# Moving set-up work of a linear attention into the loop before it, and reordering the opening of two joined attentions

## The chip, the cores and the metric

One Trainium2 chip, one core. The metric is the device time of one execution in microseconds; the median over the runs is compared. A core has five engines with their own instruction queues: TensorE (PE in the profile, its weight loads PEld), VectorE (DVE), ScalarE (ACT), GpSimd (POOL) and SyncE (SP). They meet only at semaphores: an instruction waits until a counter has reached a value that another engine's instructions raise.

## The reference

The input x has 32 sequences of 64 tokens with 128 channels, 2048 rows of 128 in all, which the kernel keeps in SBUF as 16 tiles of 128 rows. Six layers follow, each a sum of x and something of its layer norm (`_ln` here): a cross attention with 16 wide heads, a linear attention with an MLP, a mixture of four small self attentions in which each token takes part in two, a cross attention with 16 heads of 8 channels, an attention with relative positions, and a causal attention with a mixture of MLPs.

```python
x = x + cross_wide(_ln(x), ctx)                  # stage_cross_wide
x = x + linear_and_mlp(_ln(x))                   # stage_linear, stage_mlp
x = x + experts_attention(_ln(x))                # stage_two_attentions, first half
x = x + cross_narrow(_ln(x), ctx, mask)          # stage_two_attentions, second half
x = x + relative_attention(_ln(x))
x = x + causal_attention_and_moe(_ln(x))

# linear_and_mlp(x), x already normalised; rms(x, s) = x * s * (sqrt(128) + 1e-6) / |x|
q, k, v = split(rms(x, scale1) @ qkv_w.T);  q, k = exp(-q*q/2), exp(-k*k/2)
out = q @ (k.T @ v) / (q @ k.sum + 1e-6)         # per head
x = x + gamma * (out @ proj_w.T + proj_b)
return x + gamma * (gelu(rms(x, scale2) @ conv1_w.T + conv1_b) @ conv2_w.T + conv2_b)

# experts_attention(x): logits = x @ router_w + router_b; probs = softmax(logits)
# top2 experts of each token; for each expert, attention among its tokens; summed with weight probs
```

## The kernel before

The stages run one after another (`stages` in `build`). Each stage is an `nc.Block` with one instruction stream per engine, written out by hand; between two blocks all engines meet. No planner orders the work: an engine does its stream in the order of the calls, and a call such as `phi(a)` starts with the waits that it needs. `run_units` (line 97) calls `step(a)` for each unit; inside it `a.plus(1)` or `a.plus(-2)` names the unit that a call works on, so that several units are in flight. Calls outside the range of units do nothing.

**`stage_cross_wide`** (line 482) works on units of 64 query rows, two to a tile, 32 in all. Per unit TensorE makes scores in PSUM, VectorE takes maxima, subtracts them and later sums (`at.shift`, lines 353 and 358, `sums`, line 702), ScalarE does the exponential (line 364), GpSimd multiplies with the reciprocal (`scale`, line 549), TensorE transposes (line 376), ScalarE copies (line 386), TensorE multiplies with the context and, for every second unit, with the output weights (line 636); `finish` (line 712) adds the result to X. VectorE and GpSimd have idle time in each unit. At the end the last tiles run without new units beside them.

**`stage_linear`** (line 736) works on 8 groups of two tiles. VectorE first makes weights scaled by gamma and scale1 (line 770, `scaled_weights`), `stats` of the first groups (lines 788 and 794), GpSimd `scales` (lines 877 to 881), VectorE `xnorm` (lines 805 and 807: the normalised rows Xmid and the doubly normalised rows xn), and only then TensorE's `turn` (line 977) can begin. In the loop a step is: `qkv` (lines 1006 and 1008), ScalarE's `phi` (lines 946 to 958), `sums` (line 988), VectorE's `mask` (line 818), `numer` (line 1020), `divide` (lines 831 to 837), `oturn`, `proj`, `mid`. GpSimd adds `biases` (line 890) and, in steps 2 to 6, makes `constants` that the joined attentions need later, among them the memset of Vbd (line 900) and the casts of `place` (line 910).

**`stage_mlp`** (line 1049) has 8 groups of two tiles as well. Beside them it makes the statistics of the next layer norm and in steps 4 and 6 the normalised rows of the first eight tiles (`next_rows`, line 1109). After it the semaphores are cleared.

**`stage_two_attentions`** (line 1300) begins with statistics and rows of the last tiles (`rows_ready`, line 1955), transposes of all rows in four groups of four tiles (`turn_rows`, line 1471, copied to XnT by ScalarE, line 1797), the router's products with N = 4 (`route`, line 1477), `keys(0)` (lines 1521 and 1768) and `queries(0)` (lines 1512 and 1842). VectorE ranks the logits (lines 1971 to 1982, `rank_columns`), TensorE turns the one-hot rows (`turn_hot`, line 1485), ScalarE copies them; `selections` (lines 1501 and 1793) spreads them, GpSimd multiplies queries (`select`, line 1361) and keys (`keys`, line 1370) with them, `values` (lines 1533 and 1777) follow, and the first `score` (lines 1549 and 1556) and `shift` (lines 1853 and 1856). Then comes a loop of 32 units, whose `normalise` takes a reciprocal (line 1940), makes a factor from it (line 1942) and multiplies the mixed values with it (line 1946).

## Time and profile before

| | us |
|---|---|
| median of 3 runs | 1072.82 (1067.55 to 1075.33) |
| the profiled execution: its time | 1074.42 |
| the profiled execution: its span | 1072.3 |

```profile
span 1072.3 us, 26858 instructions
PE 960.8 (90%) x10835; PEld 730.2 (68%) x10835; DVE 658.4 (61%) x1312; ACT 519.3 (48%) x1071; POOL 462.0 (43%) x517
PE   4899999999867787999999999997999788699994
PEclk9999999999978887999999999998999889699997
```

The span reaches from the first to the last instruction; the time has some microseconds around it. The second line gives each engine's busy time, its share of the span and its instructions. The last two cut the span into 40 slices of 26.8 us: a digit is the busy share of TensorE in tenths, and the TensorE clock that was granted, in tenths of 2.4 GHz. The cross attention lies in slices 2 to 12, the linear attention and the MLP in 12 to 15, the joined attentions from 15 on.

### The profile page before, as it was taken

To read this page: it belongs to the slowest core of one execution; us is meant where nothing else is said; L and a number is where in the kernel's file an instruction comes from. 1 tells how busy PE (TensorE), PEld (TensorE's weight loads), DVE (VectorE), ACT (ScalarE), POOL (GpSimd) and SP (SyncE) were. 2 spreads that over 40 slices of the span, in tenths; PEclk is the share of its full clock that TensorE was granted. 3 is DMA by queue.
4 is the path that set the end of the run, shared out by engine and by line. 5 is a ranking of instruction groups with operands and counts; after the bars stand their busy time and mean duration, and the time that the engine had idled before them with its cause. 6 is when DMAs were issued, how large, how long until landed. Compare 5 with 4: busy or idle time off the path is not lost. (4 is left out here: it accounts for less than half of the span.)

```text
span 1072.3 us, 26858 instructions
## 1 busy us (share of the span) xinstructions
PE 960.8 (90%) x10835; PEld 730.2 (68%) x10835; DVE 658.4 (61%) x1312; ACT 519.3 (48%) x1071; POOL 462.0 (43%) x517
## 2 busy tenths in 40 slices
PE   4899999999867787999999999997999788699994
PEld 4788888888645576888888666664356545567773
DVE  3355555555526673877889788874589757722324
ACT  2464555555414433666666566663455438242231
POOL 1123233332215453766767534423145266356243
PEclk9999999999978887999999999998999889699997
DMA  9300034000000000000000000003963010012336
GB/s 276 143 2 1 1 90 111 1 1 1 1 1 1 1 25 17 2 3 2 3 2 2 2 2 2 2 2 115 380 192 103 2 42 4 27 49 64 90 108 181
DMA packets 43369, 55.04 MB, mean 51 GB/s; under 512 B 4368, under 2 KB 34704, under 8 KB 42864
## 3 DMA queue, kind: packets, MB, share of 16 engines
q1 hardware_dynamic: 41264, 49.07, 14.5%
q0 software_dynamic: 1984, 4.26, 1.2%
q8 instruction: 87, 1.43, 0.5%
q14 instruction: 34, 0.28, 0.1%
HBM read 30.13 MB, written 23.19 MB: 50 GB/s over the span
## 5 line engine op out<-in xcount | busy, mean ns | idle before, releaser
L549 POOL TENSOR_TENSOR c_P<-c_P,c_rl 128x1024 f32<-128x1024 f32 x32 | 60.7, 1896 | 127.5 <-DVE c_rl L705 127.5
L1741 ACT COPY e_PT<-probsT 128x512 f32<-128x512 f32 x128 | 68.8, 591 | 81.2 <-PE probsT L1570 81.2
L602 PEld LDWEIGHTS mixed<-c_xs,c_AQ 128*128 128x128 f32 x512 | 66.1, 197 | 35.1 <-issue 33.4
L702 DVE TENSOR_REDUCE c_rl<-c_P 128x8 f32<-128x1024 f32 x32 | 39.0, 1220 | 81.9 <-ACT c_P L364 81.9
L1750 ACT ACTIVATE e_P<-e_P 128x512 f32<-128x512 f32 x128 | 74.6, 641 | 0.7 <-DVE e_P L1856 0.3
L602 PE MATMUL mixed<-c_xs,c_AQ 128*128 128x128 f32 x512 | 71.3, 286 | 2.9 <-ACT c_GT L667 1.6
L626 PE MATMUL mixed<-c_PT,c_cs 128*128 128x512 f32 x128 | 68.9, 620 | 4.5 <-ACT c_RT L676 3.1
L676 ACT COPY c_RT<-mixed 128x512 f32<-128x512 f32 x64 | 37.5, 586 | 63.1 <-PE mixed L626 63.1
L1570 PE MATMUL probsT<-W,e_P 128*128 128x128 f32 x512 | 67.5, 275 | 0.0
L636 PEld LDWEIGHTS mixed<-c_VO,c_RT 128*128 128x128 f32 x512 | 60.5, 198 | 5.3 <-ACT c_RT L676 5.3
L636 PE MATMUL mixed<-c_VO,c_RT 128*128 128x128 f32 x512 | 62.1, 282 | 2.0 <-ACT c_RT L676 2.0
L612 PE MATMUL scores<-ctxT,c_GT 128*128 128x128 f32 x512 | 63.3, 277 | 0.0
L353 DVE TENSOR_REDUCE c_mx<-scores 128x8 f32<-128x1024 f32 x32 | 38.5, 1204 | 38.7 <-PE scores L612 38.7
L612 PEld LDWEIGHTS scores<-ctxT,c_GT 128*128 128x128 f32 x512 | 59.6, 192 | 2.3 <-issue 2.3
L1570 PEld LDWEIGHTS probsT<-W,e_P 128*128 128x128 f32 x512 | 57.0, 141 | 0.6
L1853 DVE TENSOR_REDUCE e_mx<-scores 128x16 f32<-128x1024 f32 x32 | 39.2, 1224 | 25.4 <-PE scores L1556 25.4
L386 ACT COPY c_PT<-probsT 128x512 f32<-128x512 f32 x64 | 34.3, 593 | 41.1 <-PE probsT L376 41.1
L667 ACT COPY c_GT<-mixed 128x256 f32<-128x256 f32 x128 | 41.4, 375 | 26.4 <-PE mixed L602 26.4
L1661 PEld LDWEIGHTS mixed<-e_V,e_PT 128*64 128x64 f32 x1024 | 32.5, 138 | 26.4 <-ACT e_PT L1741 25.6
L1895 DVE TENSOR_REDUCE e_mx<-scores 128x8 f32<-128x1024 f32 x32 | 39.0, 1219 | 15.3 <-PE scores L1641 14.9
L2935 POOL DMA_INDIRECT hbm_results<-e_yo,e_ids x30 | 28.8, 959 | 44.1 <-DVE e_yo L2910 38.6
L2093 POOL TENSOR_TENSOR u_RK<-u_KT,W 128x1024 f32<-128x1024 f32 x16 | 30.4, 1902 | 39.3 <-PE scores L2170 36.5
(391 smaller groups left out, 2377.3 us busy)
## 6 DMA issues: line engine op xcount, KB each, us to landing
hbm_dist<-u_Z SPq DMA_DIRECT2D x16, 768.0 KB, 7.5
u_S<-hbm_dist SPq DMA_DIRECT2D x64, 128.0 KB, 2.9
hbm_results<-c_blank SPq DMA_DIRECT2D x1, 3072.0 KB, 14.4
e_w<-in_w SPq DMA_DIRECT2D x12, 256.0 KB, 2.7
e_dT<-hbm_results SPq DMA_DIRECT2D x12, 256.0 KB, 4.5
W<-in_wpack SPq DMA_DIRECT2D x1, 2489.0 KB, 12.8
hbm_slots<-c_blank SPq DMA_DIRECT2D x6, 350.0 KB, 5.9
e_xin<-hbm_slots SPq DMA_DIRECT2D x6, 350.0 KB, 3.6
```

The source lines that it names most:

```text
L549: pool.tensor_tensor(pr, pr, bc(rl[:, a.up, :].unsqueeze(2), [P, PAIRS, KEYS]), ALU.mult).then_inc(s["scaled"], 1)
L602: last = pe.matmul(bank[:, (h % 4) * P:(h % 4 + 1) * P], AQ[:, h, :], xs[:, a.par, :], start=True, stop=True)
L612: last = pe.matmul(K.psS[a.up][:, c * KEYS:(c + 1) * KEYS], GT[:, a.par, a.u, 2 * c:2 * c + 2, :].rearrange("p h q -> p (h q)"), K.ctxT[:, ...
L626: pe.matmul(K.psO[:, :], cs[:, a.up, :], at.PT[:, a.up, r * 512:(r + 1) * 512], start=True, stop=True).then_inc(s["read"], 1)
L636: last = pe.matmul(K.psO[:, 0:D], RT[:, a.par, h, :], VO[:, h, :], start=(h == 0), stop=(h == HEADS - 1))
L667: last = act.copy(GT[:, a.par, b, 4 * r:4 * r + 4, :], bank[:, :].rearrange("p (h b q) -> p h b q", h=4, b=TB)[:, :, b, :])
L702: dve.tensor_reduce(rl[:, a.up, :], at.P[:, a.up, :].rearrange("p (g k) -> p g k", g=PAIRS), AX.X, ALU.add).then_inc(s["chain"], 1)
L1570: last = pe.transpose(K.psT[:, i * P:(i + 1) * P], Pr[:, n % 2, i * P:(i + 1) * P], K.ident)
L1741: act.copy(PT[:, n % 2, half * 512:(half + 1) * 512], K.psT[:, half * 512:(half + 1) * 512]).then_inc(s["tcopied"], 1)
L1750: act.activation(Pr[:, n % 2, cols], Pr[:, n % 2, cols], ACT.Exp, scale=0.5 if n < TOTAL else CSCALE).then_inc(s["exped"], 1)
L1853: dve.tensor_reduce(top, sc, AX.X, ALU.max).then_inc(s["maxed"], 1)
L1895: dve.tensor_reduce(top, sc, AX.X, ALU.max).then_inc(s["maxed"], 1)
```

## The change

Three stages are touched.

1. Linear attention. The scaled weights, the ones and zeroes of vb, and for tiles 0 to 11 the statistics and scales are made in the loop of the cross attention (`linear_weights`, `group_stats`, `linear_scale`), in named steps, four tiles at a time; also the normalised rows of tiles 0 to 3 (`linear_rows`, steps 28 and 29). The last four tiles' statistics follow in step 0 of the linear attention, their scales in its step 1. `constants` moves from GpSimd's steps 2 to 6 of the linear attention to its steps 22 to 26 of the cross attention, unchanged but for the step numbers; onehot and identb move to VectorE's steps 5 and 7 there. TensorE's first two turns wait for nothing. The buffers concerned are reserved earlier.
2. MLP. TensorE transposes the first eight tiles' rows for the joined attentions (`next_turn`, steps 5 and 7), ScalarE copies them to XnT (`next_copy`), TensorE makes their router products (`next_route`, steps 6 and 8).
3. Joined attentions. The opening is reordered as the diff shows: keys first, only the last eight tiles turned and routed there, the hot rows ahead of the first queries' bias, the exponential of the logits behind the first values, the first score ahead of the second selection, the token weights behind the first shift. In `normalise` the reciprocal is written to a free column in PSUM instead of to the SBUF tile rl, which is gone.

```diff
+def linear_scale(pool, K, s, g, count):
+    L, tiles = K.L, slice(4 * g, 4 * g + 4)
+    var = L.mv[:, tiles, 1]
+    pool.wait_ge(s["var"], count)
+    pool.tensor_scalar(L.rs[:, 0, tiles], var, LN_EPS, None, ALU.add)
+    pool.tensor_scalar(L.rs[:, 1, tiles], var, D / RMS_NUM ** 2, None, ALU.mult).then_inc(s["vareps"], 1)
+    pool.wait_ge(s["vareps"], count)
+    pool.tensor_tensor(L.rs[:, :, tiles], L.rs[:, :, tiles], K.nhalf[:, 0:8].rearrange("p (a b) -> p a b", a=2),
+                       ALU.pow).then_inc(s["rs"], 1)
+def linear_rows(dve, K, n):
+    L = K.L
+    for i in range(2):
+        t = 2 * n + i
+        mean, row_in = L.mv[:, t, 0:1], K.X[:, t, :]
+        dve.tensor_scalar(K.Xmid[:, t, :], row_in, mean, L.rs[:, 0, t:t + 1], ALU.subtract, ALU.mult)
+        last = dve.tensor_scalar(L.xn[:, n % 2, i, :], row_in, mean, L.rs[:, 1, t:t + 1], ALU.subtract, ALU.mult)
+    return last
...
                     pool.tensor_copy(w(name), byhead[:, :, :, :, :].rearrange("p g j e d -> p (g j e d)")).then_inc(s["heads"], 1)
+                def constants(n):
...
                 def step(a):
                     if a.u == 0:
                         tile_in(a.plus(2 * U))
                     context(a.plus(1))
                     scale(a.plus(1))
+                    constants(a.n)
+                    if a.n in (11, 19, 27):
+                        linear_scale(pool, K, ln, (a.n - 11) // 8, (a.n - 11) // 8 + 1)
...
+                def linear_weights(n):
+                    gamma = K.row("gamma")
+                    if n == 9:
+                        dve.wait_ge(K.load["rest"], 16)
+                        dve.tensor_scalar(L.Wqkv[:, :], w("qkvT"), w("scale1"), None, ALU.mult)
+                        dve.memset(L.vb[:, :, :, :], 0.0).then_inc(ln["zeroed"], 1)
+                    if n == 11:
...
+                        dve.tensor_tensor(L.projG[:, :], w("projT"), gamma, ALU.mult)
+                        dve.tensor_tensor(L.projB[:, :], K.row("proj_b"), gamma, ALU.mult)
...
                 def step(a):
                     at.shift(dve, a.plus(1))
...
                     if a.u == 1:
                         finish(a.plus(-2))
+                    if a.n == 5:
+                        dve.tensor_reduce(K.onehot[:, :], K.ident.rearrange("p (r i) -> p i r", r=4), AX.X, ALU.add).then_inc(
+                            s["onehot"], 1)
+                    if a.n == 7:
+                        dve.tensor_copy(K.identb[:, :], K.ident)
+                    linear_weights(a.n)
+                    if a.n in (10, 18, 26):
+                        g = (a.n - 10) // 8
+                        dve.wait_ge(ln["xout"], 4 * (g + 1))
+                        group_stats(dve, ln, L.st6, L.mv, K.X, g)
+                    if a.n in (28, 29):
+                        dve.wait_ge(ln["rs"], 1)
+                        linear_rows(dve, K, a.n - 28)
...
+                    if a.n == GROUPS - 2:
+                        dve.wait_ge(s["rs"], 1)
+                    wait(dve, s["turned"], a.n - 1)
+                    linear_rows(dve, K, a.n).then_inc(s["xn"], 1)
+                def last_stats():
+                    for t in range(TILES - 4, TILES):
+                        last = dve.bn_stats(L.st6[:, t, :], K.X[:, t, :])
+                    last.then_inc(s["stats"], 1)
+                    dve.wait_ge(s["stats"], 1)
+                    for t in range(TILES - 4, TILES):
+                        last = dve.bn_aggr(L.mv[:, t, :], L.st6[:, t, :])
                     last.then_inc(s["var"], 1)
-                def xnorm(a):
...
-                    dve.wait_ge(s["rs"], a.n + 1)
...
                 def biases(a):
                     if not inside(a):
                         return
-                    pool.wait_ge(s["xn"], a.n + 1)
+                    wait(pool, s["xn"], a.n - 1)
...
                 def step(a):
-                    scales(a.plus(2))
                     biases(a)
...
-                pool.wait_ge(s["weights"], 6)
+                    if a.n == 1:
+                        linear_scale(pool, K, s, 3, 1)
...
                         return
-                    pe.wait_ge(s["xn"], a.n + 1)
+                    wait(pe, s["xn"], a.n - 1)
                     wait(pe, s["xnT"], a.n)
...
+                def next_copy(g):
+                    act.wait_ge(v["turned"], g + 1)
+                    act.copy(K.XnT[:, 512 * g:512 * g + 512], K.psM[:, :]).then_inc(v["copied"], 1)
...
                 def step(a):
                     gelu(a)
                     xT(a.plus(1))
+                    if a.n in (5, 7):
+                        next_copy((a.n - 5) // 2)
...
+                def next_turn(g):
+                    pe.wait_ge(v["normed"], g + 1)
+                    pe.wait_ge(v["boe"], 1)
+                    wait(pe, v["copied"], g)
+                    for i in range(4):
+                        last = pe.transpose(K.psM[:, i * P:(i + 1) * P], K.Xmid[:, 4 * g + i, :], K.ident)
+                    last.then_inc(v["turned"], 1)
+                def next_route(g):
+                    pe.wait_ge(v["copied"], g + 1)
+                    for t in range(4 * g, 4 * g + 4):
+                        pe.matmul(K.psO[:, t * E0:(t + 1) * E0], K.XnT[:, t * P:(t + 1) * P], w("rw"), start=True, stop=True)
...
                     if a.n == 1:
                         bias_products()
+                    if a.n in (5, 7):
+                        next_turn((a.n - 5) // 2)
+                    if a.n in (6, 8):
+                        next_route((a.n - 6) // 2)
...
-            keyed = lambda t: M if t else K.psO
+            keyed = lambda t: M if t else K.psS[0][:, 0:512]
+            turned_rows = lambda g: K.psS[1][:, 512 * (g - DONE):512 * (g - DONE) + 512]
...
-                    turn_rows(0)
-                    turn_rows(1)
-                    route(0)
                     keys(0)
+                    for g in range(DONE, groups):
+                        turn_rows(g)
+                    for g in range(DONE, groups):
+                        route(g)
                     queries(0)
-                    route(1)
-                    for g in range(2, groups):
-                        turn_rows(g)
-                    for g in range(2, groups):
-                        route(g)
                     turn_hot()
                     selections(0)
                     values(0)
+                    score(0)
                     selections(1)
                     queries(1)
-                    score(0)
                     keys(1)
                     for n in range(TOTAL):
...
-                    for g in range(groups):
-                        act.wait_ge(q["turned"], g + 1)
-                        act.copy(K.XnT[:, g * G * P:(g + 1) * G * P], K.psS[g % 2][:, 0:G * P]).then_inc(q["copied"], 1)
-                        if g == 1:
-                            keys(0)
-                    act.wait_ge(q["shifted"], 1)
-                    act.activation(ex[:, :, :], ex[:, :, :], ACT.Exp).then_inc(q["exped"], 1)
+                    keys(0)
+                    for g in range(DONE, groups):
+                        act.wait_ge(q["turned"], g + 1 - DONE)
+                        act.copy(K.XnT[:, g * G * P:(g + 1) * G * P], turned_rows(g)).then_inc(q["copied"], 1)
                     act.wait_ge(q["hotT"], 1)
                     act.copy(hotT[:, :, :], K.psT[:, 512:512 + 2 * P].rearrange("p (i q) -> p i q", i=2)).then_inc(q["hotTout"], 1)
                     selections(0)
                     values(0)
+                    act.wait_ge(q["shifted"], 1)
+                    act.activation(ex[:, :, :], ex[:, :, :], ACT.Exp).then_inc(q["exped"], 1)
                     selections(1)
                     keys(1)
                     for n in range(TOTAL):
...
                         wait(dve, s["normed"], n - 1)
                         ps = mixed(n)
-                        dve.reciprocal(rl[:, n % 2, :], ps[:, :, E0 * HD]).then_inc(s["recip"], 1)
+                        dve.reciprocal(ps[:, :, E0 * HD + 1], ps[:, :, E0 * HD]).then_inc(s["recip"], 1)
                         dve.wait_ge(s["recip"], n + 1)
-                        dve.tensor_tensor(fac[:, n % 2, :, :], bc(rl[:, n % 2, :].unsqueeze(2), [P, HEADS, E0]),
+                        dve.tensor_tensor(fac[:, n % 2, :, :], bc(ps[:, :, E0 * HD + 1:E0 * HD + 2], [P, HEADS, E0]),
                                           bc(wsel[:, t, k, :].unsqueeze(1), [P, HEADS, E0]), ALU.mult).then_inc(s["factor"], 1)
...
+                    def token_weights():
+                        dve.wait_ge(q["exped"], 1)
+                        ch.link(dve, dve.tensor_reduce(rx[:, :], ex[:, :, :], AX.X, ALU.add))
+                        ch.link(dve, dve.reciprocal(rx[:, :], rx[:, :]))
+                        ch.link(dve, dve.tensor_tensor(ex[:, :, :], ex[:, :, :], bc(rx[:, :].unsqueeze(2), [P, TILES, E0]), ALU.mult))
+                        for k in range(TOPK):
+                            last = dve.tensor_tensor(wsel[:, :, k, :], hot[:, :, k, :], ex[:, :, :], ALU.mult)
+                        ch.link(dve, last)
+                        dve.tensor_tensor(wtok[:, :, :], wsel[:, :, 0, :], wsel[:, :, 1, :], ALU.add).then_inc(q["weights"], 1)
...
-                    queries(0)
                     ch = Chain(q["chain"])
+                    dve.memset(less[:, :, :, :], 0.0)
                     dve.wait_ge(q["logits"], 1)
-                    ch.link(dve, dve.tensor_tensor(logits[:, :, :], K.psT[:, 512:512 + TILES * E0].rearrange("p (t e) -> p t e", t=TILES),
+                    ch.link(dve, dve.tensor_tensor(logits[:, :, :], K.psO[:, 0:TILES * E0].rearrange("p (t e) -> p t e", t=TILES),
...
-                    ch.link(dve, dve.tensor_reduce(rx[:, :], logits[:, :, :], AX.X, ALU.max))
-                    dve.tensor_tensor(ex[:, :, :], logits[:, :, :], bc(rx[:, :].unsqueeze(2), [P, TILES, E0]),
-                                      ALU.subtract).then_inc(q["shifted"], 1)
-                    rank_columns(dve, ch, rank[:, :, :], less, logits, E0)
+                    rank_columns(dve, ch, rank[:, :, :], less, logits, E0, False)
...
-                    dve.wait_ge(q["exped"], 1)
-                    ch.link(dve, dve.tensor_reduce(rx[:, :], ex[:, :, :], AX.X, ALU.add))
...
-                    ch.link(dve, last)
-                    dve.tensor_tensor(wtok[:, :, :], wsel[:, :, 0, :], wsel[:, :, 1, :], ALU.add).then_inc(q["weights"], 1)
+                    queries(0)
+                    ch.link(dve, dve.tensor_reduce(rx[:, :], logits[:, :, :], AX.X, ALU.max))
+                    dve.tensor_tensor(ex[:, :, :], logits[:, :, :], bc(rx[:, :].unsqueeze(2), [P, TILES, E0]),
+                                      ALU.subtract).then_inc(q["shifted"], 1)
...
                         shift(n)
+                        if n == 0:
+                            token_weights()
```

## Rows read from the trace of the kernel before

**Rows 1.** Windows: stretch, length, busy us of each engine (instructions), TensorE clock, DMA share, GB/s

```profile
240.00:260.00 20.00, 20.00 (x145) 16.65 (x143) 10.71 (x12) 11.34 (x25) 4.97 (x6) 1.00 0.00 1
312.00:314.00 2.00, 0.29 (x3) 0.10 (x1) 1.16 (x4) 0.00 (x0) 0.00 (x0) 1.00 0.00 0
320.00:330.00 10.00, 8.43 (x26) 6.15 (x28) 3.78 (x19) 3.28 (x10) 3.07 (x6) 0.53 0.00 0
440.00:480.00 40.00, 40.00 (x670) 33.36 (x669) 32.44 (x41) 26.27 (x58) 30.07 (x30) 1.00 0.01 3
```

**Rows 2.** Timeline, first opening: start, us, engine, line, operation, tiles, idle before with releaser

```profile
313.26 0.42 DVE L770 TENSOR_SCALAR l_Wqkv<-W 128x384 f32<-128x384 f32 x1 [0.32 <-PEq L507]
...
318.74 0.69 PE L977 MATMUL scores<-W,l_xn 128*128 128x128 f32 x2 [6.45 <-DVE l_xn L807]
```

**Rows 3.** Timeline of the linear attention: query products of four steps, and the stall

```profile
342.32 0.60 PE L1006 MATMUL scores<-l_xnT,l_Wqkv 128*128 128x256 f32 x2
...
343.17 2.09 DVE L805 TENSOR_SCALAR Xmid<-X,l_mv,l_rs 128x128 f32<-128x128 f32 x1
...
343.33 1.86 POOL L900 MEMSET e_Vbd<- 128x2112 f32 x1
...
350.16 0.60 PE L1006 MATMUL scores<-l_xnT,l_Wqkv 128*128 128x256 f32 x2
...
354.82 0.60 PE L1006 MATMUL scores<-l_xnT,l_Wqkv 128*128 128x256 f32 x2
...
360.11 0.60 PE L1006 MATMUL scores<-l_xnT,l_Wqkv 128*128 128x256 f32 x2
```

**Rows 4.** Timeline of the cross attention's last units: scale, its use, last shift, ScalarE's copies

```profile
278.92 1.90 POOL L549 TENSOR_TENSOR c_P<-c_P,c_rl 128x1024 f32<-128x1024 f32 x1 [3.84 <-DVE c_rl L705]
...
285.63 1.04 PE L376 MATMUL probsT<-W,c_P 128*128 128x128 f32 x8
...
288.49 1.23 DVE L353 TENSOR_REDUCE c_mx<-scores 128x8 f32<-128x1024 f32 x1 [2.01 <-PE scores L612]
...
292.65 1.06 ACT L386 COPY c_PT<-probsT 128x512 f32<-128x512 f32 x2
```

**Rows 5.** Timeline of the MLP's end: last down products and last sum

```profile
395.17 1.16 PE L1221 MATMUL probsT<-downG,m_hT 128*128 128x128 f32 x8 [0.56 <-ACT m_hT L1183]
...
396.37 0.42 DVE L1099 TENSOR_TENSOR X<-probsT,X 128x256 f32<-128x256 f32 x1 [0.77 <-PE probsT L1221]
```

**Rows 6.** Timeline of the second opening

```profile
398.08 1.94 PE L1471 MATMUL scores<-W,Xmid 128*128 128x128 f32 x8 [1.75 <-PEq L143]
...
400.85 1.11 DVE L1955 TENSOR_SCALAR Xmid<-X,n_mv,n_rstd 128x128 f32<-128x128 f32 x4 [0.47 <-POOL n_rstd L1429]
...
404.85 0.95 PE L1477 MATMUL probsT<-W,XnT 128*128 128x4 f32 x8
...
404.89 1.89 POOL L1370 TENSOR_TENSOR e_RK<-e_KT,e_pairmask 128x1024 f32<-128x1024 f32 x1 [4.08 <-ACT e_KT L1768]
...
405.66 1.07 PE L1471 MATMUL scores<-W,Xmid 128*128 128x128 f32 x8
...
407.42 1.28 ACT L1801 ACT_TABLE_LOAD   x1
...
409.73 0.23 DVE L1971 TENSOR_TENSOR e_logits<-probsT,R 128x64 f32<-128x64 f32 x1 [3.99 <-PE probsT L1477]
...
412.48 0.40 PE L1485 MATMUL probsT<-e_identb,e_hot 128*128 128x128 bf16 x2 [2.78 <-DVE e_hot L1979]
...
419.64 0.69 DVE L1842 TENSOR_TENSOR e_QT<-mixed,biasE 128x512 f32<-128x512 f32 x1 [5.90 <-PE mixed L1512]
...
423.14 1.22 DVE L1856 TENSOR_TENSOR e_P<-scores,e_mx 128x1024 f32<-128x1024 f32 x1
```

**Rows 7.** The factor product by its line (min/median/max ns; starts), and its group (busy us, mean ns)

```profile
L1942 DVE TENSOR_TENSOR e_fac<-e_rl,e_wsel x32: 224/226/1941, 432.6 to 606.9; 128x64 f32<-128x64 f32 x32
...
L1942 DVE TENSOR_TENSOR e_fac<-e_rl,e_wsel 128x64 f32<-128x64 f32 x32 | 24.2, 756 | 1.1
```

185 lines of the change are left out of this document (70 added, 115 removed).

## The prediction

> **What bounds the kernel now.** I read the slices of busy time first, then the order of time around each stage that the diff touches. In the cross attention and in the joined attentions TensorE is busy for the whole stretch at full clock [rows 1]; there an instruction moved to another engine costs nothing while its cover holds. Between the two stages, 313 to 424 us, it is not: in the ten microseconds from 320 the clock was 0.53, which is the 1.2 GHz level and a little of the 2.4 GHz one. So that stretch is read wait by wait.
>
> The reader sees three losses. **First opening:** VectorE makes weights, statistics and first rows from 313.26, and TensorE's first transpose starts at 318.74 after 6.45 us without work [rows 2]. **Fourth step of the linear attention:** its query products start at 342.32, the next ones 7.84 us later, where the step after took 4.66; a GpSimd memset of 1.86 us lies on a VectorE scale that lasted 2.09, TensorE waited for it [rows 3]. **Second opening:** from the first instruction at 398.08 to the end of the first shift at 424.36, 26.3 us [rows 6].
>
> **Part 1, the linear attention.** Everything that stood ahead of the first transpose is made earlier, and its turn waits for nothing. It starts when the block does: 318.74 − 313.26 = 5.45 us sooner [rows 2]. All later steps hang on it, so this passes through whole. The clock was still full there before, 1.00 from 312 to 314, and fell during the idle time [rows 1, 2]. At best TensorE now stays at 2.4 GHz: of its 8.43 busy us at clock 0.53 the share 0.47, 4.0 us, would go; at worst nothing, since its first steps still have gaps for ScalarE's and VectorE's work. I take 1.7, somewhat under the middle.
> The memset leaves the fourth step: 7.84 − 4.66 = 3.18 us. The casts leave the sixth and seventh: the period 5.29 at 354.82 falls to 4.66, 0.63 us [rows 3]. The statistics that leave VectorE and the scales that leave GpSimd bring nothing more: VectorE waited for TensorE in that place, and the cycle mask, row norm, transpose, numerator, divide stays. Four late tiles' statistics go into step 0, where VectorE would wait for the first products. Part 1: 5.45 + 1.7 + 3.18 + 0.63 = **11.0 us gained**.
>
> **Part 2, what the cross loop takes on.** No DMA is issued or passed, and SP's queue is unchanged. VectorE and GpSimd each get some 10 us of small operations (0.2 to 1.9 each), spread over 30 units. A unit's GpSimd scale ends at 278.92 + 1.90 = 280.82, and TensorE uses it at 285.63: 4.8 us of cover [rows 4], more than a statistics group or a memset of 1.86. GpSimd's scales wait for VectorE's statistics one unit back, with only the next unit's copy and scale queued behind. The exception is the last pair of units, in which VectorE makes the first four tiles' rows (8 scales, 0.28 each by the four in 1.11 of [rows 6]): the drain. They come just as GpSimd runs its 1.90 us scale, and [rows 3] show a VectorE scale stretched to the end of a GpSimd instruction. Then the first rows end some 3 us late, the exponential and GpSimd's next scale slip along, the second rows end near 290.0, and the last shift starts there instead of 288.49. ScalarE's copies for TensorE, at 292.65 before, come about 1.0 us late [rows 4], and nothing after them has slack. Without the collision it is 0. I take 0.9, the price nearest to the rows.
> The Trainium skill (SBUF — State Buffer, Who interferes with whom) says that a VectorE instruction in a two-port mode and GpSimd exclude each other for a whole instruction. By that rule the cost is the 1.0, without it 0; the trace agrees with it in the stretched scale.
>
> **Part 3, the MLP.** TensorE gets two groups of four transposes (8 records, 1.07 each) and two of eight route records (0.95 each) [rows 6], 4.04 us, in its last four steps. It has little idle time there: 0.56 ahead of the last down products [rows 5]. The second group also waits for the tiles' rows, which VectorE has about a microsecond earlier; queued behind that wait are the last down products, on which the stage's end hangs. ScalarE's two copies lie under the down products. TensorE then ends at 395.17 + 1.16 + 4.04 − 0.56 = 399.8, where the block ended with VectorE's 396.37 + 0.42 = 396.8. **3.0 us given back**; 2.0 if more gaps absorb it, 3.5 if the light route products let the clock fall.
>
> **Part 4, the second opening.** Keys come first. Rows of the third group are ready as before; the fourth group's, at 400.85 to 401.96, now meet GpSimd's key product of 1.89 us, which formerly began at 404.89 [rows 6]. An estimate: GpSimd starts 3.4 us in (key products 1.94, ScalarE's four copies and the waits 1.4) and holds VectorE's last two scales to 5.3, so they end near 5.6 instead of 3.9. Then a transpose group (1.07 warm, 1.94 cold, I take 1.5) and two route groups (0.95 warm, twice that cold, I take 2.3) lead to the logits at 9.4; before 409.73 − 398.08 = 11.65. From the logits to the hot transposes 2.75; three of the small operations (memset, maximum, subtraction, about 0.25 each as the logits' 0.23) leave the way: 2.0, so 11.4. From the hot transposes to the end of the first shift it was 424.36 − 412.48 = 11.9. The first score leaves that way (2.2 us: from the query add at 419.64 to the shift, whose two halves of 1.23 begin 2.5 before 424.36) and goes under ScalarE's work; in its place come the exponential with its table load, 1.28 + 0.26, which before stood where ScalarE waited anyway, and the query add of 0.69, now ahead of the shift [rows 6]: again 11.9 with a cold clock. Warm, two groups of 8 records cost 0.9 less each; I take 11.2. End: 11.4 + 11.2 = 22.6 against 26.3, **3.7 us gained**. With cold routes 25.2, so 1.1; with everything warm and no collision 19.0, so 7.3. ScalarE's wait for the shifted logits now has the second selection's copy behind it, and so the second queries; those logits are ready long before. VectorE's token weights, seven small operations at about 0.25, stand in front of the second shift and lie under the second score; GpSimd's wait for them has only the third selection behind it.
>
> **Part 5, the reciprocal in PSUM.** The factor product took 24.2 us in 32, on average 756 ns, with a median of 226 and a longest of 1941 [rows 7]: under half of them were held up, in the trace always beside a GpSimd product. At 0.23 each the change frees 16.8 us of VectorE. I cost it at 0: TensorE shows no idle time from 440 to 480 with VectorE at 32.44 of 40 us [rows 1]. If that cover is gone it is a gain, below. The same page of the Trainium skill says that an instruction with at most one SBUF input, outside two-port modes, does not contend with GpSimd. By that the stall goes; the rows show it only for the present form.
>
> **The sum.** −11.0 + 0.9 + 3.0 − 3.7 + 0 = −10.8 us. The profiled execution took 1074.42 (span 1072.3 and 2.1 around it), so it would take 1063.6; it stands 1.6 above the median of 1072.82, and against that I predict **1062.0 us**. Its own bounds: best 13.3 + 7.3 − 2.0 = −18.6, worst 9.3 + 1.1 − 1.0 − 3.5 = −5.9.
>
> **Rivals.** *A, the gains are handed back:* cold routes and collisions make the second opening worth 1.1, the drain costs 1.0, the MLP 3.5, the clock brings nothing: −5.9, **1067**. For it: the clock of 0.53 behind the first opening, and the light routes now standing ahead of two waits. Against: the waits in part 1 are gone in any case.
> *B, all warm:* TensorE holds 2.4 GHz through both openings, with the drain and the MLP as forecast: −13.3 − 7.3 + 0.9 + 3.0 = −16.7, **1056**. For it: it was at full clock when the cross attention ended.
> *C, VectorE did bound the joined attentions:* all 16.8 us count, 1062.0 − 16.8 = **1045**. Against it: [rows 1].
> *D, slower:* the place is the factor in the joined attentions. No row shows VectorE writing PSUM. From below it costs nothing; from above, each of the two operations pays what the worst stall cost, 1.94 − 0.22 = 1.72, in all 32 units. A unit takes (606.9 − 432.6)/31 = 5.6 us [rows 7], of which VectorE is idle 19%, 1.07. At 3.44 more a unit 2.37 lies bare, 76 us: **1138**. The sign turns from 1.07 + 10.8/32 = 1.41 us a unit. I keep it out of the sum, since the nearest rows, products on PSUM of 1.2 us for 1024 columns, give 16 columns far less.
> *E, the openings weren't on the way* (TensorE would only wait elsewhere): 1073. Against it: the waits named in [rows 2].
>
> **Chances.** Forecast 0.62, A 0.15, B 0.14, C 0.03, D 0.04, E 0.02. The range leaves out C, D and E and a little of the ends: 1055.5 to 1068. Runs of this kernel lie between 1067.55 and 1075.33, so about 1% (10.7 us, under 1062.1) is what can be told from no change. Half of the forecast's chance, B and C lie under that: faster 0.48; the other half, A and E, within: 0.48; slower 0.04.
>
> **What would show it.** Right: the first transpose of the linear attention within 0.7 us of the cross attention's end; the fourth step at 4.7 us; factor products all near 0.23; the last down products of the MLP about 2.5 us later against its start; the first shift 22 to 23 us behind the second opening. Wrong: a cross loop longer by over 1 us, clock 0.5 through the first steps, idle time of TensorE in the joined attentions, or a second opening of 25 us.

## The result, and the profile after

Thirteen runs of the changed kernel have a median of 1063.78 us (1059.98 to 1067.39), thirteen of the kernel before, beside them or shown above, 1073.42 (1067.55 to 1077.78). The ratio is 0.9906, 95% interval 0.9886 to 0.9925: faster, by 9.6 us. The profiled execution after took 1066.6 (span 1064.5), which is 2.8 above its median, so the two traces are read stage by stage and not by their ends. Up to the first output product of the joined attentions (`out`, the product with the output weights; line 1602 before) the changed kernel is 11.5 us ahead (445.80 against 434.31); in later stages, which the change does not touch, it falls back to 8.3 at TensorE's last product and to 7.9 at the end of the span. The kernels below drift there too, from 4.5 us lost (e8) to 2.5 gained (e10) against the kernel before. But six of the nine with the whole change take 629 us or more from that product to the end, where the five with none or a part of it take 625.5 to 628.0. Single executions can't tell whether the change costs something there, so this stays open.

Windows of the changed kernel (stretch, length, busy us of PE, PEld, DVE, ACT and POOL, TensorE clock, DMA share, GB/s), against [rows 1]:

```profile
320.00:330.00 10.00, 8.66 (x53) 6.13 (x51) 7.12 (x31) 6.10 (x17) 2.83 (x4) 1.00 0.01 2
360.00:367.50 7.50, 6.86 (x21) 5.16 (x22) 3.50 (x19) 3.40 (x6) 3.96 (x8) 0.50 0.00 0
440.00:480.00 40.00, 40.00 (x670) 33.36 (x669) 26.95 (x41) 26.27 (x58) 29.05 (x29) 1.00 0.01 2
```

The linear attention now runs at 1.00 (2.4 GHz), the MLP's first steps at 0.50 (1.2 GHz). The joined attentions' TensorE is as full as before, though VectorE has 5.5 us less to do in 40.

Timeline around the first opening (start, us, engine, line, operation, tiles, idle before with releaser), against [rows 2 to 4]:

```profile
279.25 1.90 POOL L594 TENSOR_TENSOR c_P<-c_P,c_rl 128x1024 f32<-128x1024 f32 x1 [3.83 <-DVE c_rl L774]
279.30 1.93 DVE L512 TENSOR_SCALAR l_xn<-X,n_mv,n_rstd 128x128 f32<-128x128 f32 x1
...
286.86 1.90 POOL L594 TENSOR_TENSOR c_P<-c_P,c_rl 128x1024 f32<-128x1024 f32 x1 [4.89 <-DVE c_rl L774]
286.97 1.93 DVE L783 TENSOR_TENSOR X<-X,c_yb 128x128 f32<-128x128 f32 x1
...
289.60 0.33 DVE L512 TENSOR_SCALAR l_xn<-X,n_mv,n_rstd 128x128 f32<-128x128 f32 x1
289.86 1.21 DVE L353 TENSOR_REDUCE c_mx<-scores 128x8 f32<-128x1024 f32 x1
...
293.39 1.05 ACT L386 COPY c_PT<-probsT 128x512 f32<-128x512 f32 x2
...
314.01 0.41 PE L993 MATMUL scores<-W,l_xn 128*128 128x128 f32 x2 [0.99 <-PEq L552]
...
328.87 0.60 PE L1022 MATMUL scores<-l_xnT,l_Wqkv 128*128 128x256 f32 x2
...
333.54 0.60 PE L1022 MATMUL scores<-l_xnT,l_Wqkv 128*128 128x256 f32 x2
```

Twice a VectorE operation lasts as long as GpSimd's scale beside it: the second of the first rows, at 279.30, and the sum of X, at 286.97. The second rows are made ahead of the last shift, which starts 1.4 us later; ScalarE's copies come 0.74 us late and the block starts 0.73 late. Of each of these, 0.3 us stood already before (the transposes ahead of them start at 285.96, before at 285.63). Then the first turn waits for nothing but the block itself, and the fourth step takes 4.67 us instead of 7.84.

The second opening, against [rows 5, 6]:

```profile
384.67 1.14 PE L1245 MATMUL probsT<-downG,m_hT 128*128 128x128 f32 x8
...
387.94 1.91 PE L1563 MATMUL scores<-XnT,W 128*128 128x128 f32 x8 [1.35 <-PEq L143]
...
390.69 2.69 DVE L1992 TENSOR_SCALAR Xmid<-X,n_mv,n_rstd 128x128 f32<-128x128 f32 x4 [0.47 <-POOL n_rstd L1472]
391.10 1.94 POOL L1413 TENSOR_TENSOR e_RK<-e_KT,e_pairmask 128x1024 f32<-128x1024 f32 x1 [0.45 <-ACT e_KT L1806]
...
393.44 1.12 PE L1513 MATMUL scores<-W,Xmid 128*128 128x128 f32 x4 [2.05 <-DVE Xmid L1992]
...
394.35 3.42 PE L1519 MATMUL mixed<-W,XnT 128*128 128x4 f32 x16
...
397.80 0.23 DVE L2019 TENSOR_TENSOR e_logits<-mixed,R 128x64 f32<-128x64 f32 x1 [4.14 <-PE mixed L1519]
...
408.19 1.22 DVE L1890 TENSOR_REDUCE e_mx<-scores 128x16 f32<-128x1024 f32 x1
...
411.15 1.45 PE L1598 MATMUL scores<-e_RK,e_Qs 64*64 64x128 f32 x32
...
411.37 2.08 DVE L2003 TENSOR_TENSOR e_wsel<-e_hot,e_ex 128x64 f32<-128x64 bf16 x2
411.47 1.90 POOL L1413 TENSOR_TENSOR e_RK<-e_KT,e_pairmask 128x1024 f32<-128x1024 f32 x1 [7.42 <-ACT e_KT L1806]
...
413.48 1.08 DVE L2005 TENSOR_TENSOR e_wtok<-e_wsel 128x64 f32<-128x64 f32 x1
414.49 1.21 DVE L1890 TENSOR_REDUCE e_mx<-scores 128x16 f32<-128x1024 f32 x1
```

Two collisions of VectorE with GpSimd stand in it. The fourth group's rows are ready 5.4 us into the stage, behind GpSimd's key product, and TensorE waits 2.05 us for them. Singly, the four scales took 0.35, 0.34, 1.92 and 0.33 us; the third is the one that met it:

```profile
391.21 1.92 DVE L1992 TENSOR_SCALAR Xmid<-X,n_mv,n_rstd 128x128 f32<-128x128 f32 x1
```

The other collision is that of the token weights: the second score is done at 412.60, but its row maximum starts at 414.49, behind them. Between the two collisions TensorE runs at 0.50: the sixteen route products take 3.42 us.

The factor product, its group and the reciprocal's (busy us, mean ns, idle before), against [rows 7]:

```profile
L1977 DVE RECIPROCAL scores<-scores 128x16 f32<-128x16 f32 x31 | 7.9, 256 | 0.0
...
L1979 DVE TENSOR_TENSOR e_fac<-scores,e_wsel 128x64 f32<-128x64 f32 x31 | 7.0, 225 | 1.1
```

### The profile page after: what moved, and what is told of

Same layout as the page of the kernel before. It is cut to its first block and busy times, and to the rows that moved or that the text cites. A ratio compares the mean times of both kernels' runs of the same rounds, so it can differ in the third digit from the quotient of the medians.

```text
span 1064.5 us, 26826 instructions
## 1 busy us (share of the span) xinstructions
PE 960.5 (90%) x10835; PEld 729.9 (69%) x10835; DVE 645.4 (61%) x1312; ACT 520.1 (49%) x1071; POOL 459.3 (43%) x505
```

## The experiments

Whole runs of one kernel lie up to 10 us apart (the thirteen before), so each experiment is read at its own place. Times in the table are us from the profiled execution: the linear attention from its first turn to the MLP's first turn; the MLP from there to its last down product; then, from that product, the starts of the first, second and fourth row maximum and of the first output product of the joined attentions. (The expectations call this last point the first output transpose; the transposes themselves start 4.0 us earlier in every kernel.) The ratio is to the kernel before, on the same chip, and as recorded; it isn't the quotient of two medians. A stage's time comes from one execution of each kernel, and these were not equally lucky: those of e1 and e4 were the lowest of their kernel's runs, those of the changed kernel and of e7 the second highest, that of e12 the highest.

| kernel | linear | MLP | 1st max | 2nd | 4th | output | median, ratio [95%] |
|---|---|---|---|---|---|---|---|
| before | 53.89 | 22.54 | 26.71 | 30.61 | 40.12 | 50.63 | |
| changed | 46.03 | 24.63 | 23.52 | 29.82 | 39.13 | 49.64 | 1063.78, 0.9906 [0.9886, 0.9925] |
| e1 linear part only | 46.01 | 23.90 | 23.59 | 27.49 | 37.00 | 47.50 | 1065.81, 0.9934 [0.9908, 0.9959] |
| e2 MLP and opening only | 53.85 | 23.26 | 24.36 | 29.73 | 39.03 | 49.54 | 1075.48, 1.0011 [0.9992, 1.003] |
| e3 PSUM reciprocal only | 50.67 | 22.67 | 26.78 | 30.68 | 40.18 | 50.69 | 1075.42, 1.001 [0.9993, 1.0026] |
| e4 before, TensorE filled | 49.01 | 23.64 | 23.59 | 27.49 | 36.99 | 47.50 | 1071.5, 0.9983 [0.9966, 1.0001] |
| e5 keys late | 46.46 | 23.79 | 21.96 | 28.89 | 38.20 | 48.71 | 1063.07, 0.9894 [0.9857, 0.993] |
| e6 exponential early | 46.04 | 23.20 | 24.40 | 29.76 | 39.07 | 49.58 | 1062.68, one run |
| e7 e6, weights early | 46.03 | 24.67 | 23.31 | 28.26 | 40.29 | 50.80 | 1063.33, 0.9891 [0.9855, 0.9927] |
| e8 e5, e7, rows late | 46.05 | 23.10 | 21.70 | 26.66 | 38.67 | 49.17 | 1062.69, 0.9888 [0.9854, 0.9921] |
| e9 seam filled | 45.93 | 22.08 | 23.52 | 30.45 | 39.84 | 50.35 | 1064.29, one run |
| e10 e5, opening filled | 46.02 | 24.55 | 20.45 | 27.38 | 38.24 | 48.75 | 1060.24, 0.9878 [0.9842, 0.9915] |
| e11 e9 and e10 | 45.92 | 22.08 | 19.66 | 26.59 | 37.46 | 47.97 | 1056.93, 0.9829 [0.9804, 0.9854] |
| e12 e11 and e8 | 45.94 | 22.08 | 19.29 | 23.18 | 33.34 | 43.85 | 1054.45, 0.9809 [0.9784, 0.9833] |

### The parts alone

**e1**, the kernel before with everything that moves into the cross attention's loop:

```diff
+                    constants(a.n)
+                    if a.n in (11, 19, 27):
+                        linear_scale(pool, K, ln, (a.n - 11) // 8, (a.n - 11) // 8 + 1)
...
+                    linear_weights(a.n)
...
+                    if a.n in (28, 29):
+                        dve.wait_ge(ln["rs"], 1)
+                        linear_rows(dve, K, a.n - 28)
```

> The kernel before with the linear attention's part alone (cross loop, linear attention), no change to the MLP's work, the second opening or the factor. Theory: the linear attention shrinks by 13.3 us as in the changed kernel (5.5 wait, 3.8 memset and casts, 3.8 clock), the drain costs 0.7, the MLP up to 1.4 because its first steps fall on a cold clock: -11 to -12.5 us, ratio about 0.989. Rival: the MLP and joined attentions' part carries much of the change: then this alone gives under 8 us.

**e2**, the kernel before with the MLP's added transposes and routes and the reordered opening:

```diff
+                    if a.n in (5, 7):
+                        next_turn((a.n - 5) // 2)
+                    if a.n in (6, 8):
+                        next_route((a.n - 6) // 2)
...
-                    for g in range(2, groups):
+                    for g in range(DONE, groups):
```

> The kernel before with the MLP's early transposes and routes and the reordered second opening alone; linear attention, cross loop and factor as before. Theory: the MLP grows by 1.0 (transposes are one record each, not two), the opening to the end of the first shift shrinks by 3.6, and 2.4 of that is lost again before the second shift, since the token weights collide with GpSimd's products: net 0 to -1 us, ratio 0.999 to 1.000. Rival (the forecast's own step): nothing is lost behind the first shift and the MLP costs 3.0: -0.7; the total is the same, the places are not. Rival 2: the reordering as such is a loss, over +1.

**e3**, the reciprocal alone:

```diff
-                        dve.reciprocal(rl[:, n % 2, :], ps[:, :, E0 * HD]).then_inc(s["recip"], 1)
+                        dve.reciprocal(ps[:, :, E0 * HD + 1], ps[:, :, E0 * HD]).then_inc(s["recip"], 1)
```

> The kernel before with the reciprocal written to PSUM alone. Theory: every factor product takes 0.23 us, 17 us of VectorE time go, the execution keeps its time within 0.3 us, since TensorE bounds that loop. Rival C: VectorE bounds it, up to -16 us. Rival D: the write to PSUM costs, slower.

The linear part carries the change: 7.9 us inside its stage, and a ratio of 0.9934. The forecast of about 0.989 lies below its interval: whole runs gave less than the stages promised. (Its profiled execution took 1060.81 us against a median of 1065.81, so the later columns of its row are its best and not its usual case.) The MLP and the opening alone leave the time as it was: 0.7 us more in the MLP, 1.1 less by the first output product. The reciprocal frees VectorE and is worth next to nothing: from the first to the last output product e3 took 168.31 us, before 168.49. The factor's rows in e3 (min/median/max ns; starts) and in e2, which writes SBUF still (group: busy us, mean ns):

```profile
L1942 DVE TENSOR_TENSOR e_fac<-scores,e_wsel x31: 223/224/225, 428.2 to 596.6; 128x64 f32<-128x64 f32 x31
```
```profile
L1963 DVE TENSOR_TENSOR e_fac<-e_rl,e_wsel 128x64 f32<-128x64 f32 x32 | 24.2, 757 | 1.1
```

Two things in the table were not foreseen. e3 does not touch the linear attention, and still that stage took 3.2 us less: the granted clock was back at 1.00 between four and six us behind its first turn, before only between ten and twelve, and did not fall again in the fourth step. And e1 and e4 have the opening of before, untouched, and run it 3.1 us faster. A window in each, from about five us behind the last down product; first e1, then e3:

```profile
388.00:393.00 5.00, 4.76 (x43) 4.53 (x42) 2.47 (x8) 2.31 (x7) 2.93 (x2) 1.00 0.73 208
```
```profile
396.00:401.00 5.00, 5.00 (x29) 5.00 (x29) 1.54 (x5) 1.25 (x5) 0.93 (x2) 0.59 0.61 186
```

The same transposes and routes, once at 1.00 and once at 0.59. So the opening of before has two lengths, and the reordered one is 1.0 us shorter than the one and 2.1 longer than the other. It ran its routes at 0.50 itself, so the second comparison is not one at equal clock.

### The clock of the linear attention

**e4**, the kernel before with TensorE kept at work while it waits for the first rows:

```diff
+                for _ in range(40):
+                    pe.transpose(pY[:, 0:P], K.ident, K.ident)
                 turn(At(0, 0, 1))
```

> The kernel before with 40 transposes of the identity by TensorE into an unused bank while it waits in the first opening; their result is not used, the output is the reference's. Nothing else differs. Theory of the clock: TensorE stays at 2.4 GHz through the first steps, the first transpose starts where it did, and the linear attention shrinks by 3.8 us, ratio about 0.9965. Rival: the 3.8 us beyond the waits came from the statistics and scales that left the loop: then nothing changes.

The first turn comes 15.23 us behind the cross attention's last turn, as in the kernel before (318.74 − 303.51 and 319.07 − 303.84), and then the clock is full:

```profile
319.00:329.00 10.00, 6.67 (x34) 4.68 (x34) 5.39 (x25) 5.33 (x15) 4.89 (x9) 1.00 0.00 0
```

The stage takes 4.9 us less with nothing else changed: that is what the low clock cost in the profiled execution of before. Against e3's execution of the same stage it is 1.7. In whole runs the forecast 0.9965 lies just outside the interval [0.9966, 1.0001], which also reaches 1: the stage shows the effect, the whole time doesn't show it clear of noise. The fourth step's query products, and the next ones:

```profile
339.01 0.60 PE L1006 MATMUL scores<-l_xnT,l_Wqkv 128*128 128x256 f32 x2
...
345.23 0.60 PE L1006 MATMUL scores<-l_xnT,l_Wqkv 128*128 128x256 f32 x2
```

With the memset in place and the clock at 1.00 this step takes 6.22 us, not 7.84.

### The waits of the reordered opening

**e5**, on the changed kernel, GpSimd's key product behind VectorE's last rows:

```diff
+                    pool.wait_ge(q["normed"], groups - DONE)
```

> The changed kernel with one wait more: GpSimd starts the key product of the first block (1.94 us in the changed kernel's profile) only when VectorE has scaled the fourth group of rows. Judged from the last down product of the MLP to the first output transpose of the joined attentions, 49.64 us in the changed kernel's profile, since whole runs scatter by 4 us. Theory (port shared by VectorE and GpSimd): the scale of the third and fourth group takes 1.08 us again instead of 2.69, TensorE waits 0.4 us for the rows instead of 2.05, and all behind comes 1.6 us sooner: 48.0 us, whole kernel ratio to before 0.989. If TensorE's granted clock also stays at 1.00 over the sixteen routes (3.42 us at 0.50), 1.7 us more: 46.3 us. Rival (the rows are not what the opening waits for): the key product itself is late, VectorE's and TensorE's work behind start where they did, 49.6 us, ratio 0.9905.

```profile
386.97 1.12 DVE L1993 TENSOR_SCALAR Xmid<-X,n_mv,n_rstd 128x128 f32<-128x128 f32 x4 [0.47 <-POOL n_rstd L1472]
...
388.17 1.89 POOL L1413 TENSOR_TENSOR e_RK<-e_KT,e_pairmask 128x1024 f32<-128x1024 f32 x1 [1.24 <-DVE Xmid L1993]
```

The collision is shown: 1.12 instead of 2.69 us, logits and first maximum 1.56 sooner, as forecast (1.6). By the first output product 0.9 is left: 48.71 where 48.0 was forecast, since the token weights, beside the same GpSimd products, then stand in the way for longer (4.6 us, and 6.93 from the first to the second maximum, where the changed kernel has 6.30).

**e6** and **e7**: the table load and the exponential off ScalarE's way, then the token weights ahead of the second queries too.

```diff
+                    act.activation(Pr[:, 0, 0:1], K.nhalf[:, 0:1], ACT.Exp)
...
-                    values(0)
                     act.wait_ge(q["shifted"], 1)
                     act.activation(ex[:, :, :], ex[:, :, :], ACT.Exp).then_inc(q["exped"], 1)
+                    values(0)
...
+                    token_weights()
                     queries(1)
...
-                        if n == 0:
-                            token_weights()
```

> The changed kernel with a one-column exponential on ScalarE behind the first keys, which loads the table where ScalarE is idle, and with the exponential of the routing logits ahead of the first values instead of behind them. Theory: the table load (1.28 us) and the exponential (0.26 us) no longer stand ahead of the second block's selector copy (405.86), so its queries and the first shift behind them come 1.5 us sooner; the stretch of 49.64 us becomes 48.1 us. Rival: the first shift waits for TensorE's scores at granted clock 0.50 and not for ScalarE; the stretch stays within 0.4 us of 49.6.

> As the kernel with the early exponential, and VectorE makes the token weights ahead of the second block's queries instead of behind the first shift. Theory (the weights behind the first shift stand in the way: there they took 2.08 + 1.08 us beside GpSimd's products, and the second shift started 3.8 us behind the first one's end): they take their undisturbed 1.2 to 1.5 us in VectorE's idle time of 6.8 us ahead of the first shift, and the second shift comes 2 us sooner; with the table load the stretch of 49.64 us becomes 46.1 us, ratio to before 0.987. Rival (the second shift waits for TensorE's second score at a low clock): only the part of the early exponential is left, 48.1 us or none of it, 49.6 us.

e6 goes the rival's way, at 49.58 us. Its selector copy starts where it did, 21.1 us behind the last down product, now waiting for TensorE; its clock stood at 0.50 for longer than the changed kernel's, so what the edit gives at an equal clock isn't shown:

```profile
405.20 0.48 ACT L1831 CAST e_sel<-mixed 128x384 bf16<-128x384 f32 x1 [1.54 <-PE mixed L1543]
```

e7 misses its 46.1 and both rivals by going the other way, to 50.80. It brings the second maximum 1.6 us forward and the fourth 1.2 us back: a wait for VectorE became idle time of TensorE, and the clock, 0.95 from 27 to 30 us behind the last down product in the changed kernel and 1.00 from there, was back only between 33 and 36 here (0.80).

**e8**, all of these, and in the cross loop:

```diff
-                    if a.n in (28, 29):
+                    if a.n == 30:
                         dve.wait_ge(ln["rs"], 1)
-                        linear_rows(dve, K, a.n - 28)
+                        for n in range(2):
+                            linear_rows(dve, K, n)
```

> The three edits of the opening together, and both pieces of the linear attention's rows behind the last tile's projection of the cross attention instead of between its last steps. Theory: the drain of the cross attention loses its 0.7 us, the stretch from the last down product to the first output transpose falls by 1.6 + 1.5 + 2 us to 44.5 us, the whole kernel to about 1058 us, ratio 0.985. Rival A (one of the three waits only takes the place of another, or the clock falls a stretch earlier): half of it, 1061 us, ratio 0.988. Rival B (moving the rows behind step 30 makes the first turn of the linear attention wait): the linear attention's first turn, 9.8 us behind the last cross turn, comes later by 0.7 us and the drain gives nothing.

Rival A, and worse: the first maximum is 1.8 us sooner, the second 3.2, the output product 0.5. In the cross loop the stretch between its last two turns is 9.61 us, where e5 has 10.00 and e3 and e4, with the loop of before, 9.61: the drain is gone, and the first turn of the linear attention comes 9.76 us behind that turn in both. Four removed waits did not add up while the clock was low.

### The clock again, in the changed kernel

**e9** fills the seam, **e10** the opening, **e11** both (`fill(bank, n)` is n transposes of the identity into free columns; first the two places of e9, then those of e10, which has the edit of e5 too):

```diff
+                    if a.n >= GROUPS:
+                        fill(pQ, 5)
...
+                fill(pT[0], 12)
                 turn(At(0, 0, 1))
+                fill(pT[1], 3)
```

```diff
                     def turn_rows(g):
+                        fill(K.psS[0][:, 512:1024], (10, 6)[g - DONE])
...
+                    fill(K.psT[:, 512:1024], 5)
                     queries(1)
+                    fill(K.psT[:, 512:1024], 6)
                     keys(1)
+                    fill(K.psT[:, 512:1024], 6)
```

> The changed kernel with transposes of the identity into free PSUM columns where TensorE waits around the seam of linear attention and MLP: five in each of the linear attention's last two steps, twelve ahead of the MLP's first turn, three behind it (0.11 us each at full clock, some 2.8 us of work in waits of about 3 us). Judged from the MLP's first turn to its last down product, 24.63 us in the changed kernel's profile, with the granted clock at 0.50 for the first 7.5 us of it. Theory (the 2.1 us that the MLP grew are mostly TensorE at 0.50, and TensorE's work ahead of it keeps the clock): granted clock 1.00 through the MLP's start, 22.0 us or less. Rival (the stage is held by its added transposes and routes at full clock): 24.6 us even at 1.00. Second rival: the fill does not hold the clock; 24.6 us and what the fill costs, up to 2.8 us.

> The changed kernel with the key product held back as before, and with transposes of the identity where TensorE waits in the opening of the joined attentions: ten ahead of the third group's turn, six ahead of the fourth's, five, six and six around the second block's queries and keys. From the MLP's last down product to the first output transpose: 49.64 us in the changed kernel's profile, 48.71 with the key product held back alone; the opening of before took 50.6 us where its routes ran at granted clock 0.50 and 47.5 us where they ran at 1.00. Theory (the reordered opening would be worth its 3 to 4 us, and the lower clock under it takes most of that back): granted clock 1.00 until 14 us behind the last down product or longer, and 45.5 us (47.5 less 2, since what is left of the opening's waits is shorter than before). Rival (the clock is not what holds the reordered opening; VectorE and GpSimd are): 48.7 us at any clock. Second rival: the fill costs more than it gives, 50 us.

> The fills of the seam and of the opening together, and the key product held back. Theory: the linear attention's last steps and the MLP give 2.5 us, the opening 4 us, and the whole kernel comes to about 1057 us, ratio 0.984. Rival (what the clock gives in one stretch it takes in the next, as the runs so far hint at with their 4 us of scatter): within 2 us of the changed kernel, ratio 0.989 to 0.991. Second rival: the fills cost what they take, 1066 us, ratio 0.992.

e9, the same stretch of the MLP as above:

```profile
359.50:367.00 7.50, 6.47 (x44) 5.64 (x45) 4.37 (x21) 3.93 (x8) 4.65 (x9) 1.00 0.00 0
```

44 records of TensorE in 7.5 us, three of them fill, instead of 21. The MLP falls from 24.63 to 22.08, below that of before, with all its added work. But by itself this gave the whole kernel nothing that one run could show: the opening behind it was at 0.50 again. e10 missed its 45.5: it starts its first maximum 1.5 us before e5's, and has lost that by the output product (48.75, the first rival's 48.7). Its clock wasn't held from the start, 0.55 from three to six us behind the last down product, so that rival, which speaks of any clock, isn't shown by it. e11 holds 1.00 for twelve us, and its first maximum comes 3.9 us before the changed kernel's; the whole is 1056.93, close to the forecast of 1057, though more than half of what it had won by the output product came from the seam. In the opening the forecast of 4 us failed; it was 1.7. VectorE in e11 shows where:

```profile
401.27 1.21 DVE L1911 TENSOR_REDUCE e_mx<-scores 128x16 f32<-128x1024 f32 x1
...
404.19 1.60 DVE L2022 TENSOR_TENSOR e_ex<-e_ex,e_rx 128x64 f32<-128x64 f32 x1
...
405.68 2.27 POOL L1416 TENSOR_TENSOR e_Qs<-e_QT,e_sel 128x512 f32<-128x512 f32 x2
405.83 2.20 DVE L2024 TENSOR_TENSOR e_wsel<-e_hot,e_ex 128x64 f32<-128x64 bf16 x2
...
408.20 1.21 DVE L1911 TENSOR_REDUCE e_mx<-scores 128x16 f32<-128x1024 f32 x1
```

At full clock the second score is ready at 405.1, and the token weights, stretched beside GpSimd's products, keep its maximum waiting for 3.1 us.

**e12** puts the edits of e8 into e11, and one fill more:

```diff
+                        if n == 1:
+                            fill(K.psS[1], 6)
                         score(n + 1) if n + 1 < TOTAL else wide_score(0)
```

> The kernel with all fills, and in it the early exponential, the token weights ahead of the second block's queries, both pieces of the linear attention's rows behind the cross attention's last projection, and six more transposes of the identity ahead of the third score. In the kernel with all fills the first row maximum of the joined attentions started 19.66 us behind the last down product, the second 6.93 us behind the first, the fourth 6.5 us behind the third, and the first output transpose came at 47.97 us. Theory (the token weights between first and second maximum cost 2 us also at full clock, and the late low clock 1.1 us): gaps of 4.96 and 5.4 us in their place, the output transpose at 44.9 us, the cross attention's drain 0.4 us shorter, the whole kernel at 1053.5 us, ratio 0.980. Rival (the work moved ahead of the first maximum delays it by what it saves behind it, or the clock falls in another place): the output transpose at 47 to 48 us, the whole kernel at 1056.5 us, ratio 0.983.

```profile
400.98 1.22 DVE L1915 TENSOR_REDUCE e_mx<-scores 128x16 f32<-128x1024 f32 x1
...
404.87 1.23 DVE L1915 TENSOR_REDUCE e_mx<-scores 128x16 f32<-128x1024 f32 x1 [1.42 <-PE scores L1617]
```
```profile
396.00:410.00 14.00, 11.87 (x175) 9.90 (x174) 9.04 (x13) 6.55 (x14) 7.65 (x7) 1.00 0.01 1
```

The gap between the maxima is 3.9 us, the clock 1.00 from nine us behind the last down product on, and the output product comes at 43.85 (forecast 44.9), 5.8 us before the changed kernel's. The median is 1054.45 (forecast 1053.5), 1.9% under the kernel before; the two ratios make it 0.990 of the changed kernel (0.987 to 0.993, their intervals combined, since the two weren't timed side by side). From e11 whole runs don't tell it apart: the intervals overlap. Its six runs lie within 2.1 us (1054.34 to 1056.39), where the changed kernel's thirteen spread over 7.4.

## Why the prediction held, step by step

**Part 1 (−11.0).** From block start to MLP start the stage fell from 56.77 to 43.48 us: −13.3. The first turn came 5.46 us sooner, as forecast (the difference of its two starts is 5.48; 5.45 is a slip). The rest is split by e4: the clock alone gives 4.9 (53.89 to 49.01), against 1.7, and what leaves the loop gives 3.0 at full clock (49.01 to 46.03), against 3.81. The clock is the mis-sized term. I took the middle of a bound made from ten us at 0.53; it was more than the bound's 4.0, since the clock of before was still low beyond those ten us (0.77 from 324 to 336), and low again in the fourth step (0.59 from 346 to 350.2). So the 3.18 put on the memset were only in part its price: that step came at 4.67 as forecast, but with the memset and a full clock it takes 6.22 and the one behind it 5.05, which makes 1.95 over two steps of 4.66. e3 shows that before's own clock varies there: part of the term is the luck of the profiled execution.

**Part 2 (+0.9).** The block starts 0.73 us later, but 0.35 of that stood at the first transposes of the stage (48.58 against 48.23), before the loop had taken on anything. The drain itself cost 0.4, under half of the forecast, through the last shift, as reasoned. The first rows did meet GpSimd's scale (279.30, 1.93 us), and nothing waited for them. What moved the last shift was the sum of X ahead of the second rows, 1.93 us where it took 0.32 before, together with those rows. e8 takes the 0.4 back.

**Part 3 (+3.0).** Block +2.42. The size is nearly right and its make-up is wrong. I had counted eight records for four tiles, but the eight of 1.07 us in [rows 6] are two groups: four tiles take four records, 0.60 and 0.66 us in the changed MLP. e2 prices the added work at 0.72 with the clock of before, e1 the low clock at the MLP's start at 1.36 without the added work; together 2.08, and the changed kernel has 2.09 (24.63 − 22.54). What I took for work is two thirds clock in this execution. e9 confirms it, and so do e6 and e8, which have the same MLP and took 23.20 and 23.10 us where the clock was back sooner.

**Part 4 (−3.7).** From the block's start to the end of the first shift: 410.66 − 387.94 = 22.7 us, forecast 22.6, and rows at 5.4 us, forecast 5.6. On the way small errors cancel: the sixteen routes took 3.42 us at 0.50 where 2.3 were taken, and the hot transposes started at 11.8, not 11.4; from there it was 10.9, not 11.2. But the step "token weights … lie under the second score" failed. The score was done 1.9 us before its maximum could start. Of 3.6 us won, 2.4 are gone at the second shift, and the first output product is 1.0 us nearer to the last down product than before. Against the opening of before at full clock (e1, e4) it is 2.1 farther. (The weights are six operations; the prediction counted seven.) e2's ratio, 1.0011, says the same: reordered, the opening won nothing that a run could show.

**Part 5 (0).** e3: ratio 1.001 [0.9993, 1.0026], with the factor at 224 ns and VectorE freed of about 17 us. C and D fall with it. The Trainium skill (SBUF — State Buffer, Who interferes with whom) says that an instruction with at most one SBUF input, outside the two-port modes, does not contend with GpSimd; the trace agrees, with no factor product above 226 ns in the changed kernel, against 1941.

**The sum.** −13.3 + 0.7 + 2.4 − 3.6 + 2.4 = −11.4 at the second shift, forecast −10.8; in whole runs −9.6, so that the median, 1063.78, lies 1.8 above the 1062.0. The nearness is in part luck, for the misses cancel: the clock gave 3.2 us more than I took, what left the loop 0.8 less, and the token weights took 2.4. Rival B's clock held in the linear attention only; rival A's cold routes and rows behind the key product held in the opening. E falls: the waits were on the way.

**What stays open.** How much the linear part alone is worth beside the whole change: 0.9934 and 0.9906 have intervals that overlap. Why the clock fell at the opening of before in two profiled executions and not in e1 and e4 can't be told from single executions. The end of the cross attention has two lengths in the same way: in six of the fourteen kernels its last two turns lie 9.6 to 10.0 us apart at 1.00, in eight 12.5 to 12.9 with some six us at 0.50, and e3 and before, on opposite sides, have the same code there. e12 gives back 1.6 us at its last output product, again by the clock: behind the same wait of 1.29 us its fifteenth output product took 1.98 us at 0.55, e11's 1.16 at 1.00.

## What to carry to other kernels

Between two dense stages TensorE's clock decides what a removed wait is worth: four edits moved the output product by 0.5 us at a low clock (e8), and three of them with one fill more by 4.1 where the clock was held (e12 against e11; 3.0 of it between the first and second maximum, 1.1 between the third and fourth, ahead of which the fill stands). These are single executions, and fills in one place alone (e9, e10) did not do it. So fill TensorE's waits with harmless transposes first, and then take away the waits that still stand. And before small VectorE operations are hidden under a matrix product, look at what GpSimd does in that place: in e11 it stretched six small operations over 4.6 us.

## What the runs showed of the hardware

Transposes of the identity, 0.11 us apart at full clock, held the granted clock at 1.00 in the seam in all three kernels that had them; in the opening ten and six held it in e11, but not from the start in e10 and e12, where it was 0.55 and 0.63 in the second three us and back at 1.00 by the fourth. ScalarE's table load cost 1.28 us, with the exponential 0.02 behind it. In three of the collisions above VectorE's operation began 0.05 to 0.11 us behind GpSimd's and ended some 0.1 behind its end: those at 279.30, 286.97 and 391.21, beside GpSimd's at 279.25, 286.86 and 391.10. The two scales of the fourth group that began ahead of GpSimd's product, at 390.69 and 390.96, took their 0.35 and 0.34. In [rows 3] the scale at 343.17 began 0.16 us ahead of the memset, but inside the GpSimd product before it (342.66 to 343.39), and ended 0.08 behind the memset: it was held over both.
